# Query, key and output projections as three products of high and low parts, in another order of the loop

## The reference

```
c  = layernorm(x + relu(x@W1[lang] + b1)@W2[lang] + b2) * gamma + beta   # adapter of the block's language
q  = c @ Wq.T        # 16 heads of 16 features
k, v = c @ Wk.T, c @ Wv.T            # one head of keys and values, shared
p  = softmax(mask(q k.T / 4))        # causal
x1 = x + (p v) @ Wf.T + bf
y  = expert_layer(x1)                # 256 -> 1024 -> 256, part of it by an expert per block
out = x1 + ffn(y)                    # 256 -> 1024 -> 1024 -> 1024 -> 256
```

## Time and profile before

| | us |
|---|---|
| median of 3 executions | 1118.78 (1117.38 to 1119.62) |
| the profiled execution | 1118.38 |
| its span, first to last instruction | 1116.4 |
| TensorE busy in the span | 1093.7 (98%), granted clock full in every slice |
| VectorE, ScalarE, GpSimd busy | 785.6, 586.6, 173.9 |

### The profile page before, as it was taken

The page is one execution under the profiler, slowest core; times in us unless marked ns, Lnnn a source line. Parts: engine busy times, 40 slices in busy tenths (PEclk is TensorE's granted clock), DMA queues, the critical chain, the costliest instruction groups (busy, mean ns, idle before and its releaser), DMA issues.

```text
span 1116.4 us, 18106 instructions
## 1 busy us (share of the span) xinstructions
PE 1093.7 (98%) x5979; PEld 862.5 (77%) x5995; DVE 785.6 (70%) x1378; ACT 586.6 (53%) x988; POOL 173.9 (16%) x192
## 2 busy tenths in 40 slices
PE   7899999999989999999999999999999999999998
PEld 4577677776757888888888888888888888888886
DVE  3867777777787557755688765888748777577875
ACT  2456566565656444532556564655636565455653
POOL 2122223222353543431000000000000000000000
PEclk9999999999999999999999999999999999999999
DMA  7445656557745655645134531245421454304421
GB/s 173 81 89 117 110 123 114 113 115 162 230 118 188 225 177 206 215 164 208 38 132 151 170 132 56 96 149 169 151 75 44 163 169 151 113 11 140 150 94 39
DMA packets 82255, 148.57 MB, mean 133 GB/s; under 512 B 15504, under 2 KB 42016, under 8 KB 82080
## 3 DMA queue, kind: packets, MB, share of 16 engines
q1 hardware_dynamic: 72690, 126.92, 40.1%
q10 hardware_dynamic: 9518, 21.11, 5.3%
HBM read 107.63 MB, written 30.41 MB: 124 GB/s over the span
## 4 chain that ended last, share of the span: by engine, by line
PE 93%; DVE 3%; DMA 1%; ACT 1%; issue 1%; SPq 1%; POOL 0%; ACTq 0%; DVEq 0%; POOLq 0%
PE bank L1720 36%; PE bank L1682 11%; PE bank L1434 7%; PE bank L1732 5%; PE bank L1352 4%; PE bank L1658 4%; PE bank L1652 4%; PE bank L1371 3%; PE bank L1318 3%; PE bank L1390 3%; PE bank L1426 2%; PE bank L1355 2%; PE bank L1286 1%; PE bank L1298 1%; PE bank L1410 1%; DMA q_t<-q_high 1%
## 5 line engine op out<-in xcount | busy, mean ns | idle before, releaser
L1720 PE MATMUL bank<-op_hi,w_ring 128*128 128x512 f32 x896 | 348.6, 389 | 0.0
L1720 PE MATMUL bank<-op_lo,w_ring 128*128 128x512 f32 x896 | 348.6, 389 | 0.0
L1179 DVE TENSOR_TENSOR op_lo<-x_blk,op_hi 128x512 fp32r<-128x512 f32 x288 | 193.7, 684 | 30.4 <-ACT op_hi L839 30.3
L839 ACT ACTIVATE op_hi<-x_blk 128x512 fp32r<-128x512 f32 x288 | 162.8, 620 | 73.5 <-PE bank L1720 69.3
L1720 PEld LDWEIGHTS bank<-op_hi,w_ring 128*128 128x128 f32 x896 | 168.2, 188 | 35.1
L1720 PEld LDWEIGHTS bank<-op_lo,w_ring 128*128 128x128 f32 x896 | 168.1, 188 | 34.9
L962 DVE TENSOR_REDUCE neg_max<-bank 128x2 f32<-128x512 f32 (+1 forms) x192 | 124.7, 685 | 32.4 <-PE bank L1355 30.3
L646 ACT ACTIVATE p<-bank 128x512 f32<-128x512 f32 x192 | 108.9, 596 | 37.9 <-PE bank L1371 33.6
L863 ACT ACTIVATE x_blk<-x_blk,scales 128x512 f32<-128x512 f32 x96 | 69.3, 722 | 67.0 <-DVE x_blk L1232 28.9
L1682 PE MATMUL bank<-tile_hi,ffn_w 128*128 128x512 f32 x256 | 101.6, 397 | 0.0
L541 POOL TENSOR_SCALAR_AFFINE_SELECT p<-p 128x512 f32<-128x512 f32 (+1 forms) x96 | 76.2, 794 | 158.8 <-ACT p L646 158.7
(11 more groups left out here) (127 smaller groups left out, 1731.5 us busy)
## 6 DMA issues: line engine op xcount, KB each, us to landing
w_ring<-hid_scratch SPq DMA_DIRECT2D x112, 512.0 KB, 4.6
hid_scratch<-comb ACTq DMA_DIRECT2D x8, 1792.0 KB, 7.8
q_t<-q_high SPq DMA_DIRECT2D x64, 128.0 KB, 4.7
comb<-in_hid_d ACTq DMA_DIRECT2D x6, 768.0 KB, 4.9
xt<-in_x_t SPq DMA_DIRECT2D x16, 256.0 KB, 3.4
xtok<-in_x_tok SPq DMA_DIRECT2D x16, 256.0 KB
resid<-in_x_t SPq DMA_DIRECT2D x16, 256.0 KB, 3.0
q_t<-q_rest SPq DMA_DIRECT2D x32, 128.0 KB, 4.5
```

Of the source, the lines that this page charges most:

```text
L839: nc.scalar.activation(op_hi[:, o % OP_RING, k], x_blk[:, operand_home(o), k], ACT.Copy).then_inc(s["op_hi"], 1)
L1179: nc.vector.tensor_tensor(op_lo[:, o % OP_RING, k], x_blk[:, operand_home(o), k], op_hi[:, o % OP_RING, k].bitcast(F32), ALU.subtract).the ...
L1720: last = mm(banks[first_bank + m][:, :], w, read(v[:, q % OP_RING, k, :]), start=k == 0 and v is op_hi and i not in (P2, P3), stop=k == KB ...
```

## The change

Query, key and value, and output weights are split once into a high and a low float32r part. The raw weights are loaded into memory that is used later for other things. For each block ScalarE rounds the transposed norm to a high part (`norm_parts`), VectorE subtracts it to get the low part (`norm_rest`); `attention_out` now writes the high part directly and VectorE gets the low part from the bank (`attention_low`). The projections multiply weight high * value high, weight low * value high, then wait for the low part and multiply weight high * value low. TensorE's, VectorE's and ScalarE's lists are put in another order, and SyncE's `store_x1` moves behind `move_maxima` and `load_resid`.

```diff
@@ ScalarE
             def affine(n):
                 act.wait_ge(s["norm_t_mm"], n + 1)
+                if not is_first(n):
+                    act.wait_ge(s["norm_low"], n)
...
+            def norm_parts(n):
+                act.wait_ge(s["norm_t_out"], n + 1)
+                if not is_first(n):
+                    act.wait_ge(s["kv_mm"], n)
+                nc.scalar.activation(norm_high[:, :, :], norm_t[:, :, :], ACT.Copy).then_inc(s["norm_hi"], 1)
@@ ScalarE, iteration 0: norm_parts(b + 2) behind affine(b + 2); iterations from 1
                 if front:
                     affine(b + 2)
+                    norm_parts(b + 2)
                 if softmax:
                     exponential(b, 4)
+                    exponential(b, 5)
                 if front:
                     queries_high(b + 2)
                 if softmax:
-                    exponential(b, 5)
                     exponential(b, 6)
-                    exponential(b, 7)
                 if tail:
                     attention_out(b - 1)
+                if softmax:
+                    exponential(b, 7)
+                    exponential(b, 8)
                 if front:
                     keys_copied(b + 2)
                 if softmax:
-                    exponential(b, 8)
                     exponential(b, 9)
@@ VectorE
+            def norm_rest(n):
+                dve.wait_ge(s["norm_hi"], n + 1)
+                nc.vector.tensor_tensor(norm_low, norm_t[:, :, :], norm_high[:, :, :].bitcast(F32), ALU.subtract).then_inc(s["norm_low"], 1)
+
+            def attention_low(b):
+                dve.wait_ge(s["att_t_out"], b + 1)
+                nc.vector.tensor_tensor(att_low, side[1][:, :].rearrange("p (k t) -> p k t", k=KD), att_t[:, :, :].bitcast(F32),
+                                        ALU.subtract).then_inc(s["att_low"], 1)
+
+            def split_queries_weights():
+                dve.wait_ge(s["const_loaded"], 80)
+                nc.vector.tensor_copy(wq_high, wq_raw).then_inc(s["wq_hi"], 1)
+                dve.wait_ge(s["wq_hi"], 1)
+                nc.vector.tensor_tensor(wq[:, :, :], wq_raw, wq_high.bitcast(F32), ALU.subtract).then_inc(s["weights_split"], 1)
...
@@ VectorE, iteration -1: norm_rest(b + 2) behind maximum 0; iteration 0: behind maximum 4, and at its end
                     keys_low(b + 2, (slot + 2) % SLOTS)
-                    dve.wait_ge(s["out_loaded"], 32)
+                    split_out_weights()
@@ VectorE, iterations from 1
                 if maxima:
                     maximum(b + 1, 2)
                     maximum(b + 1, 3)
+                    maximum(b + 1, 4)
+                    maximum(b + 1, 5)
+                if front:
+                    norm_rest(b + 2)
                 if tail:
                     attention(b - 1, 1)
                 if softmax and not maxima:
                     check_first_chunk()
                     split_fc2a()
                 if maxima:
-                    maximum(b + 1, 4)
-                    maximum(b + 1, 5)
                     maximum(b + 1, 6)
+                    maximum(b + 1, 7)
                 if front:
                     queries_low(b + 2)
                 if maxima:
-                    maximum(b + 1, 7)
                     maximum(b + 1, 8)
                     maximum(b + 1, 9)
+                if tail:
+                    attention_low(b - 1)
+                if maxima:
                     maximum(b + 1, 10)
                     maximum(b + 1, 11)
                     split_maxima(b + 1)
@@ VectorE, block 0
             add_adapted(0)
+            split_queries_weights()
             normalise(0)
+            split_keys_weights()
+            norm_rest(0)
             queries_low(0)
@@ VectorE, first tile of phase two
+                    if is_first(t) and m == 5:
+                        attention_low(B - 1)
@@ TensorE
             def project_queries(n, tail):
-                pe.wait_ge(s["norm_t_out"], n + 1)
+                pe.wait_ge(s["norm_hi"], n + 1)
...
+                for w in (wq_high, wq):
+                    for m in range(KD):
+                        for k in range(KD):
+                            mm(ring[0][:, m * T:(m + 1) * T], w[:, k, m * P:(m + 1) * P], norm_high[:, k, :], start=w is wq_high and m == 0 and k == 0, stop=False)
+                pe.wait_ge(s["norm_low"], n + 1)
                 for m in range(KD):
                     for k in range(KD):
-                        last = mm(ring[0][:, m * T:(m + 1) * T], wq[:, k, m * P:(m + 1) * P], norm_t[:, k, :], start=k == 0, stop=k == KD - 1)
+                        last = mm(ring[0][:, m * T:(m + 1) * T], wq_high[:, k, m * P:(m + 1) * P], norm_low[:, k, :], start=False, stop=m == KD - 1 and k == KD - 1)
...
```

More of the change, by code:

```diff
@@ L213, in build @@
         p1 = sb("p1", [P, 2, 2, 4, P], F32, one)
-        wf = sb("wf", [P, KD, D], F32, one)
+        wf = sb("wf", [P, KD, D], F32R, one)
         bf = sb("bf", [P, KD], F32, one)
@@ L767, in _ @@
             affine(0)
+            norm_parts(0)
             act.wait_ge(s["const_loaded"], 80)
@@ L1326, in project_keys @@
                     pe.wait_ge(s["values_out"], 2 * n)
-                for k in range(KD):
-                    last = mm(ring[1][:, 0:T], wkv[:, k, :], norm_t[:, k, :], start=k == 0, stop=k == KD - 1)
+                if is_first(n):
+                    pe.wait_ge(s["weights_split"], 2)
+                passes = [(w, v, k) for w, v in ((wkv_high, norm_high), (wkv, norm_high), (wkv_high, norm_low)) for k in range(KD)]
+                for i, (w, v, k) in enumerate(passes):
+                    last = mm(ring[1][:, 0:T], w[:, k, :], v[:, k, :], start=i == 0, stop=i == len(passes) - 1)
                 last.then_inc(s["kv_mm"], 1)
@@ L1423, in project_out @@
                     pe.wait_ge(s["norm_t_out"], b + 4)
+                for w in (wf_high, wf):
+                    for m in range(KD):
+                        for k in range(KD):
+                            mm(side[0][:, m * T:(m + 1) * T], w[:, k, m * P:(m + 1) * P], att_t[:, k, :], start=w is wf_high and m == 0 and k == 0, stop=False)
+                pe.wait_ge(s["att_low"], b + 1)
                 for m in range(KD):
                     for k in range(KD):
-                        last = mm(side[0][:, m * T:(m + 1) * T], wf[:, k, m * P:(m + 1) * P], att_t[:, k, :], start=k == 0, stop=k == KD - 1)
+                        last = mm(side[0][:, m * T:(m + 1) * T], wf_high[:, k, m * P:(m + 1) * P], att_low[:, k, :], start=False, stop=m == KD - 1 and k == KD - 1)
                 last.then_inc(s["proj_mm"], 1)
@@ L1544, in iteration @@
                     max_scores(b + 1, ahead, 1)
+                if softmax:
+                    scores(b, slot, 0)
                 if tail:
@@ L1565, in iteration @@
                 if maxima:
-                    max_scores(b + 1, ahead, 4)
+                    max_scores(b + 1, ahead, 5)
                 if softmax:
@@ L1569, in iteration @@
                 if maxima:
-                    max_scores(b + 1, ahead, 5)
+                    max_scores(b + 1, ahead, 6)
                 if front:
@@ L1573, in iteration @@
                 if maxima:
-                    max_scores(b + 1, ahead, 6)
+                    max_scores(b + 1, ahead, 7)
+                if tail:
+                    attention_transposed(b - 1)
                 if softmax:
```

80 lines of the change are left out of this document (47 added, 33 removed).

## The result

The changed kernel takes 1126.86 us, the median of 10 executions (1122.16 to 1129.19); the kernel before, measured beside it, 1119.38 (10 executions, 1117.38 to 1123.77). Ratio 1.0058, 95% interval 1.0043 to 1.0073: slower by 7.5 us, where 1118.8 was forecast and 1122.4 was the upper end. The profiled execution took 1127.22 us, span 1125.3, 8.9 above that of before.

What follows compares the result with a forecast made beforehand. The chain looked 93% TensorE, but each iteration begins on VectorE, both paths ending nearly together. Terms +2.6 - 4.8 + 0.3 - 0.1 + 2.3 - 0.3 = 0.0 gave 1118.8 us, range 1114.8 to 1122.4 (own range 1117.2 to 1120.4).

Steps and rivals of the forecast that it cites:

- the new order of SyncE's issues: Moves of queries and maxima: no limit inside an iteration, costed at nothing; 0.4 us if uncovered.
- the split of `wf`: End of iteration 0: VectorE splits wf behind keys_low, 0.42 + 0.69 us and handoffs, with TensorE waiting until 57.6.
- The head: Up to iteration 1's start: added copies and the wait for wf cost +2.6 us, bounds +1.8 and +3.2.
- Iterations 1 to 12: Steady iterations: period 19.3 us against 19.71, 0.4 less each, -4.8 us in all.
- the old tail: End of an iteration: from maximum 10 to the next adapter_in, 3.1 us as in the kernel before.
- my walk: One iteration traced from adapter_in: VectorE's series gives 19.4 us, TensorE's path 19.2, so 19.3 was taken.
- The head of iteration 14: First maxima wait for moved queries, whose projection ends later: +0.3 us, with no gain from iteration 13.
- Iteration 15: Output projection's last four products wait for attention_low behind check_first_chunk and split_fc2a: +2.3 us, bounds +1.3 and +2.5.
- single waits are covered: Rival: iteration 15's wait or wf's is taken up behind, 1.8 to 2.4 us back, about 1116.6; chance 0.10.
- TensorE's path binds: Rival: in iterations 1 to 12 VectorE has more room, period 19.04, total -3.2, 1115.6 us; chance 0.20.
- Fills 10 and 11 come late: Rival: maxima 10 and 11 late for VectorE lengthen each iteration; 0.3 us late gives 1122.4; chance 0.25.
- the signs that I had named for being wrong: Periods of 19.1 us or less or 19.6 or more, or either single wait under 1 us.

Runs made afterwards that it cites:

- e7: Changed kernel with all its waits kept, but TensorE multiplying idle operands during them; 1121.55 us, ratio 1.0019.
- e12: e6 without the output projection's third product, and GpSimd's selection of scores 8 and 9 waiting for the split of the maxima; 1109.34 us, ratio 0.9908.
- e11: e6 plus idle multiplications in iteration -1, and GpSimd's selection of scores 8 and 9 waiting for the split of the maxima; 1112.09 us, ratio 0.9938.
- e1: Changed kernel with only SyncE's order put back, store_x1 ahead of move_maxima and load_resid; 1122.40 us, ratio 1.0025.
- e6: Changed kernel with the edits of e1, e2 and e3 together; 1113.55 us, ratio 0.9943.
- e2: Changed kernel with only TensorE's wait for the split weights moved from the end of iteration 0 into project_out; 1121.71 us, ratio 1.0022.
- e3: Changed kernel with only iteration 15's VectorE order changed: split_fc2a, attention_low, then check_first_chunk; 1125.53 us, ratio 1.0050.

## Why the prediction was wrong

Two steps failed. The sum put the new order of SyncE's issues at nothing, and it cost 2.75 us at the head of iteration 14 (point 3). The sum had no term for the half clock behind the new stops, and it cost 5.25 us (points 1, 2, 4 and 5). A third, smaller miss is the split of `wf`, 1.2 us too cheap (point 1). Together that is 9.2; the sum missed 8.85, since the steady iterations gave a little more than forecast.

1. **The head, +2.6 against +5.73**, outside its bounds of 1.8 to 3.2. The mechanism was right (TensorE stands for the split of `wf`), the size was not. `keys_low`, behind which the split stands, starts 2.60 us later than before (57.30 against 54.70), where the sum had 0.7: 0.75 is block 0, where the sum had 0.6 for the projection's end; 1.34 is iteration -1, with the first half-clock stretch (in e7 it is 0.12); the rest is iteration 0. From the end of `keys_low` to `adapter_in` it takes 60.74 - 58.33 = 2.41 us, where the sum had 1.2. The rows of the split are these (VectorE, then GpSimd), 0.03 us behind `keys_low`:

```profile
57.30 1.03 DVE L991 TENSOR_TENSOR keys<-kv,keys 32x256 fp32r<-32x256 f32 x2
58.36 0.43 DVE L984 CAST tile_hi<-comb 128x512 fp32r<-128x512 f32 x1
58.82 1.46 DVE L986 TENSOR_TENSOR wf<-comb,tile_hi 128x512 fp32r<-128x512 f32 x1
...
58.62 1.11 POOL L550 TENSOR_SCALAR_AFFINE_SELECT p<-p 128x1024 f32<-128x1024 f32 x1 [1.02 <-ACT p L663]
```

   I had priced the subtraction at 0.69 and it took 1.46: it met the selection that runs from 58.62 to 59.73. Another 0.46 us lie between its end and TensorE's start; the profile names no releaser for them, and their cause stays open. The earlier trace rows had this very spread, 0.69 to 1.67, and I weighed it for `norm_rest` alone, where it never occurred (median of its 16 instances 0.68 us, longest 0.78). The rule that I cited there from the Trainium skill, "SBUF — State Buffer", section "Who interferes with whom" (a VectorE instruction with two SBUF inputs and a GpSimd instruction that reads SBUF contend, and the later one is blocked), agrees in kind with both places where the runs show it: 0.77 us here, 0.4 in `split_maxima`. In size it does not quite: had the subtraction waited for the selection's end and then run its full 0.69 or 0.19 us, it would have ended some 0.15 us later than it did in both places (an estimate from the rows; the selection's own times are rough).

2. **Iterations 1 to 12.** The period of 19.3 was right within 0.07 and the start of the queries right (188.95 - 177.77 = 11.18 us in, 11.2 forecast); four multiplications take 0.47, 0.118 each. But the binder was not one that I named: a third path, from scores 8 and 9 through the exponential and GpSimd's selection to VectorE's subtraction, ended last. It was hidden inside the 3.1 us that I carried over from the old tail as one lump. That lump holds 0.57 us of subtraction where it takes 0.19 alone, which is why my walk put VectorE's series at 19.4 and e12 has it at 18.98; that the number came out right is partly luck. TensorE's path, 19.2 in the walk, was right (19.21 in e11). And the half clock in iteration 1, 1.65 by e7, took a third of the term.

3. **The head of iteration 14, +0.3 against +3.05: the first step that failed.** I followed the queries' own dependence and wrote that `move_maxima`, freed of `store_x1`, covered the rest. I did not ask what the store was moved in front of: the copy that releases the load of the feed-forward weights. That load then goes out later and lands later, and the queries' moves, issued behind it, land later too. e1 puts the store back and the stop goes.

4. **Iteration 15, +2.3.** The stop is there (2.23 us where 2.7 were forecast, ended by VectorE), and e6 against e1 puts its cost at 2.54. In e1, which has the stop and no half clock in this stretch, the whole stretch is 44.92 against 43.06 us: +1.86, as the sum had it (+1.9). What the +4.15 of the changed kernel has beyond that is the two half-clock stretches, 2.38 by e7.

5. **The half clock: the second step that failed.** The sum had no term for it: TensorE's clock in before's profile was 1.00 throughout, and I treated new stops as costing their length. e7 shows some 5 us of the 7.5 to be this. Not every stop brings it: in e1 TensorE stood 2.23 us in iteration 15 and the clock stayed at 1.00. Nor is it the length of a stop alone: ahead of the norm and of the first maxima of iteration -1 the kernel before stood 1.29 and 1.18 us and stayed at 1.00, and the changed kernel stood 1.29 and 1.32 and fell to 0.50. What decides between them no run here shows.

The rival "single waits are covered" had the sign wrong. "TensorE's path binds" was not far from the order of paths in e11, though at 19.21 and not 19.04. "Fills 10 and 11 come late" named a slower outcome for a cause that did not happen: maximum 10 starts 16.27 us into an iteration (194.04 - 177.77), where its slot was. Of the signs that I had named for being wrong none appeared (the period is neither under 19.1 nor over 19.6, both single waits are over 1 us): they watched the mechanisms that I had, and both failed steps were ones that I lacked.

## What to carry to other kernels

A new single wait of a full TensorE costs its length and may cost over a microsecond more in granted clock behind it (1.2 to 1.7 us a stretch here); mend it by placing the wait where the operand is first read (e2), or by making the operand earlier (e3). When an order of DMA issues changes, list what each queue holds behind the moved one, not only what waits for it. When two paths seem to set a period and shortening either brings nothing, look for an instruction whose duration, not its start, depends on another engine.

## What the runs showed of the hardware

- VectorE's subtraction of 128x32 with both inputs in SBUF took 0.19 us alone and 0.56 to 0.67 when a GpSimd selection had started up to 0.11 us before it; it ended 0.03 to 0.05 us behind the selection. The 128x512 subtraction took 1.46 us instead of 0.69 under a selection of 128x1024.
- The granted clock fell to 0.50 (1.2 GHz) behind stops of TensorE of 3.17, 4.35 and 2.23 us and behind a pair of 1.29 and 1.32 us with 0.63 us of work between them (changed kernel); multiplications on idle operands in those stops kept it at 1.00 (e7). It stayed at 1.00 behind a stop of 2.23 us in e1 and behind a pair of 1.29 and 1.18 us in the kernel before.
- A multiplication of 256 columns with its own stationary tile took 0.118 us between float32r tiles and 0.43 us (two records of 0.216) between float32 tiles, both at a granted clock of 1.00.
